# Attention bodies 0 to 4: the gathered expert rows weighted and added by GpSimd instead of VectorE

## What is computed

```python
    x = L0_attn_x
    x = x + 0.5 * _L0_ffn_ref(_layernorm(x, axis=-1), ...)
    x = x + _L0_attn_ref(_layernorm(x, axis=-1), ...)
...
        topk_w, topk_idx = jax.lax.top_k(probs, TOP_K)      # TOP_K = 2 of 8 experts
...
        out = jnp.sum(out * weights[..., None], axis=1)
```

```python
        attn = jax.nn.softmax(jnp.einsum('bhqd,bhkd->bhqk', q, k) * scale, axis=-1)
        out = jnp.einsum('bhqk,bhkd->bhqd', attn, v)
```

## Time and profile before

| | us |
|---|---|
| median of 3 runs | 1469.15 |
| lowest, highest | 1468.4, 1480.79 |
| the profiled execution | 1480.3 |
| its span, first to last instruction | 1478.6 |
| mean granted TensorE clock | 0.951 of full |

### The profile page before, as it was taken

The page is one execution under the profiler, slowest core; times in us unless marked ns, Lnnn a source line. Parts: engine busy times, 40 slices in busy tenths (PEclk is TensorE's granted clock), DMA queues, the critical chain, the costliest instruction groups (busy, mean ns, idle before and its releaser), DMA issues.

```text
span 1478.6 us, 20417 instructions
## 1 busy us (share of the span) xinstructions
PE 1279.2 (87%) x6496; PEld 771.1 (52%) x6496; DVE 1152.3 (78%) x2430; ACT 886.1 (60%) x1402; POOL 517.3 (35%) x757
## 2 busy tenths in 40 slices
PE   5579989778999869979778999989999889899998
PEld 5357768512222322322266777766666345666665
DVE  6377879789999989898456989878786664787875
ACT  5467667437888858868666676733433467434432
POOL 6653326454534524522243334533530110200100
PEclk9779999969999999999989999999999999999999
DMA  8432264342222212210061122263644011055344
GB/s 286 111 96 67 82 214 144 108 123 85 65 67 85 82 46 71 86 36 23 16 257 51 50 72 79 71 151 83 135 90 99 8 32 27 0 117 116 87 88 115
DMA packets 88679, 133.94 MB, mean 91 GB/s; under 512 B 16756, under 2 KB 42836, under 8 KB 87548
## 3 DMA queue, kind: packets, MB, share of 16 engines
q1 hardware_dynamic: 81404, 117.93, 28.3%
q0 software_dynamic: 7168, 14.69, 3.4%
HBM read 82.23 MB, written 47.45 MB: 88 GB/s over the span
## 4 chain that ended last, share of the span: by engine, by line
PE 53%; DVE 24%; issue 9%; ACT 6%; DMA 3%; another core or an unknown queue 1%; POOL 1%; SPq 1%; DVEq 0%; ACTq 0%; POOLq 0%
PE bank L1545 6%; DVE shared L2155 5%; PE pair L894 5%; PE pair L896 5%; PE pair L895 5%; PE bank L2233 4%; PE pair L1457 3%; PE pair L1459 3%; PE pair L1458 3%; DVE shared L950 3%; PE pair L2215 3%; PE pair L2147 3%; ACT shared L2223 2%; DMA shared<-p_coef_rows 1%; PE bank L964 1%
## 5 line engine op out<-in xcount | busy, mean ns | idle before, releaser
L2155 DVE TENSOR_REDUCE shared<-pair 128x2 f32<-128x1024 f32 x256 | 309.7, 1218 | 35.9 <-PE pair L2147 32.7
L2223 ACT ACTIVATE shared<-pair 128x1024 f32<-128x1024 f32 x256 | 260.5, 1021 | 56.8 <-PE pair L2215 54.5
L950 DVE TENSOR_TENSOR shared<-shared 128x512 fp32r<-128x512 f32 x232 | 194.3, 846 | 99.6 <-ACT shared L940 63.2
L894 PE MATMUL pair<-shared 128*128 128x512 f32 x464 | 202.6, 437 | 21.6 <-issue 11.4
L1512 ACT ACTIVATE shared<-pair 128x512 f32<-128x512 f32 x144 | 85.6, 595 | 179.0 <-PE pair L1459 170.1
L896 PE MATMUL pair<-shared 128*128 128x512 f32 x464 | 190.8, 411 | 0.0
L895 PE MATMUL pair<-shared 128*128 128x512 f32 x464 | 190.8, 411 | 0.0
L935 ACT ACTIVATE shared<-pair,shared 128x512 f32<-128x512 f32 x168 | 115.8, 689 | 73.3 <-PE pair L896 67.9
L1457 PE MATMUL pair<-shared 128*128 128x512 f32 x288 | 154.0, 535 | 5.1 <-DVE shared L1467 5.1
L635 POOL DMA_INDIRECT xs_rows<-shared,slots x112 | 114.1, 1019 | 83.6 <-issue 26.9
L2233 PE MATMUL bank<-shared 128*9 128x512 f32 x1024 | 135.9, 603 | 4.5 <-ACT shared L2223 3.7
(11 more groups left out here) (380 smaller groups left out, 2262.2 us busy)
## 6 DMA issues: line engine op xcount, KB each, us to landing
shared<-p_coef_rows SPq DMA_DIRECT2D x64, 512.0 KB
shared<-xs_rows SPq DMA_DIRECT2D x42, 256.0 KB
ys_rows<-shared SPq DMA_DIRECT2D x42, 256.0 KB
w_keep<-shared SPq DMA_DIRECT2D x8, 1024.0 KB
shared<-w_keep SPq DMA_DIRECT2D x16, 512.0 KB
shared<-p_q_parts SPq DMA_DIRECT2D x64, 96.0 KB
shared<-p_k_parts SPq DMA_DIRECT2D x64, 96.0 KB
xs_rows<-shared SPq DMA_DIRECT2D x1, 5376.0 KB, 18.1
```

The costliest lines, as they stand in the source:

```text
L894: nc.tensor.matmul(out_bank, w_hi, x_hi, start=start, stop=False)
L950: nc.vector.tensor_tensor(hl[u % RING][:], hid[u % RING][:], hh[u % RING][:], ALU.subtract).then_inc(s["dve_done"], 1)
L2155: nc.vector.tensor_reduce(mneg[:, i, 2 * c:2 * c + 2], pair_of("max", b, m)[:], AX_X, ALU.max, negate=True).then_inc(s["mx_read"], 1)
L2223: nc.scalar.activation(probs[st % 2][:, 2 * p:2 * p + 2, :], pair_of("exp", b, 2 * st + p)[:], ACT.Exp, scale=scale).then_inc(s["exp_done" ...
```

## The change

In bodies 0 to 4 VectorE's eight fused operations go. GpSimd does the combine in two halves, one for each of the two experts. A half multiplies four 128x128 tiles of the gathered rows in place by the tokens' weights (L321), waits for its own last multiplication (a new semaphore, `scaled`), and adds the four tiles to x by one 128x512 addition (L327), which reports to `x_mix`. The second half's addition also waits for the first's. The first half stands behind the fifth gather and ahead of the split of q, the second behind the last split of maxima and ahead of the split of k. The combine of sequences 0 to 2, outside these bodies, stays on VectorE. The streams of TensorE, ScalarE and SP are the same.

```diff
--- before.py
+++ after.py
@@ -153,7 +153,7 @@
         x_first, x_rest, w_loaded = sem("x_first"), sem("x_rest"), sem("w_loaded")
         rows_loaded, tables_ready = sem("rows_loaded"), sem("tables_ready")
         pool_chain, vecs_ps, vecs_ready = sem("pool_chain"), sem("vecs_ps"), sem("vecs_ready")
-        x_upd, x_mix = sem("x_upd"), sem("x_mix")
+        x_upd, x_mix, scaled = sem("x_upd"), sem("x_mix"), sem("scaled")
         y_stored = [sem(f"y_stored{i}") for i in range(2)]
         gathered = [sem(f"gathered{i}") for i in range(2)]
         xn_ready, xnT_ps, xnT_ready = sem("xn_ready"), sem("xnT_ps"), sem("xnT_ready")
@@ -311,20 +311,20 @@
                 last.then_inc(x_mix, 1)
                 v.wait_ge(x_mix, 2 * (B * occ + b) + k + 1)
 
-        def combine_piece(v, occ, b, j):
-
-            k, i = divmod(j, TILES)
-            t = b * TILES + i
-            if j == 0:
+        def combine_pool(g, occ, b, k):
+
+            if k == 0:
                 per = B // 2 - 1 + b % 2
-                v.wait_ge(gathered[b % 2], 16 * 2 * TILES * (per * occ + b // 2 + b % 2))
-            if j == TILES:
-                v.wait_ge(x_mix, 2 * (B * occ + b) + 1)
-            g = staged[b % 2][:].rearrange("p k (i e) -> p (k i) e", e=E)
-            done = nc.vector.scalar_tensor_tensor(out=x_res[:, t, :], in0=g[:, 2 * i + k, :], scalar=w_tok[:, t, k:k + 1],
-                                                  in1=x_res[:, t, :], op0=ALU.mult, op1=ALU.add)
-            if i == TILES - 1:
-                done.then_inc(x_mix, 1)
+                g.wait_ge(gathered[b % 2], 16 * 2 * TILES * (per * occ + b // 2 + b % 2))
+            rows = staged[b % 2][:].rearrange("p k (i e) -> p (k i) e", e=E)
+            for i in range(TILES):
+                last = nc.gpsimd.tensor_scalar(rows[:, 2 * i + k, :], rows[:, 2 * i + k, :], w_tok[:, b * TILES + i, k:k + 1], None, ALU.mult)
+            last.then_inc(scaled, 1)
+            g.wait_ge(scaled, 2 * (b - 3) + k + 1)
+            if k:
+                g.wait_ge(x_mix, 2 * (B * occ + b) + 1)
+            both = rows.rearrange("p (i k) e -> p i k e", k=2)
+            nc.gpsimd.tensor_tensor(x_res[:, b * TILES:(b + 1) * TILES, :], x_res[:, b * TILES:(b + 1) * TILES, :], both[:, :, k, :], ALU.add).then_inc(x_mix, 1)
 
         def route_consts(g):
 
@@ -2407,16 +2407,12 @@
                 if b + FIRST < B and at == 18:
                     v_dve(v, b + FIRST, bank[7])
                 if b + AHEAD < B:
-                    if at in COMBINE_AT:
-                        combine_piece(v, occ0, b + AHEAD, COMBINE_AT.index(at))
                     if at == 24:
                         norm_stats(v, f0 + b + AHEAD, b + AHEAD)
                     if at == 25:
                         norm_aggr(v, f0 + b + AHEAD)
                 if j == 1:
                     route_dve(v, b, st)
-
-            COMBINE_AT = (13, 15, 16, 17, 19, 20, 21, 23)
 
             def dve_b(v, b, par, first_, last_):
                 for st in range(STEPS):
@@ -2468,10 +2464,14 @@
                 if routes is not None and b:
                     seq_root(g, routes, b - 1)
                 fetch((4, 12))
+                if b + AHEAD < B:
+                    combine_pool(g, occ0, b + AHEAD, 0)
                 if b + FIRST < B:
                     split_pool(g, "q", b + FIRST)
                 fetch((5, 15))
                 msplit_pool(g, b, 3)
+                if b + AHEAD < B:
+                    combine_pool(g, occ0, b + AHEAD, 1)
                 if b + FIRST < B:
                     split_pool(g, "k", b + FIRST)
                 fetch((6, 20))
```

## The result

| | before | after |
|---|---|---|
| median of 6 runs each, us | 1473.78 | 1486.3 |
| lowest, highest | 1468.4, 1480.79 | 1482.41, 1489.21 |
| ratio, 95% interval | | 1.0067 [1.0037, 1.0098] |
| profiled execution, us | 1480.3 | 1486.1 |
| its span | 1478.6 | 1484.4 |

The change makes the kernel slower by 0.67%, some 9.9 us by the ratio; the interval goes from 5.5 to 14.4 us, and the two medians lie 12.5 us apart. The six runs of before are the three that were known and three more; the median of all six is 1473.78, 4.6 us above the 1469.15 from which the forecast started.

What follows compares the result with a forecast made beforehand. No engine was full on average, but VectorE was nearly full inside an attention body, and it and TensorE delayed each other. +5.7 - 1.4 - 0.8 + 2.4 = +5.9 us took the median from 1469.15 to 1475.0, range 1464 to 1487.

Steps and rivals of the forecast that it cites:

- bodies 1 to 3, stall less pieces: TensorE's scores behind L2191 come later, less the price of VectorE's removed combine operations: 1.9 us a body, +5.7 us.
- bodies 1 to 3, clock: TensorE idles before L2191 and its granted clock falls: two falls in three bodies, 1.2 us each, +2.4 us.
- body 0: GpSimd is early before the maxima's split, so its added work hides and VectorE's removed operations show: -1.4 us.
- body 4: GpSimd is early while VectorE's routing holds TensorE back; removed combine operations gain -0.8 us, range -1.5 to 0.
- The place: L2191 in bodies 1 to 3 waits about 3 us for GpSimd's maxima split; none in bodies 0 and 4.
- load: Rival from the experiments: 7.3 us more GpSimd work a body costs wherever it stands, for instance through shared SBUF access.
- C: GpSimd time of one half, four multiplications, gaps and one addition: about 2.9 us, own range 2.6 to 3.5.
- the dear case: Rival at L2191, bodies 1 to 3: GpSimd multiplications cost 884 ns, C is 5.2, +14 us, 1483; chance 0.13.
- the rival of the absorbed stall: The pace picks up behind the stall and no clock falls: about 0 (-2 to +2), 1469; chance 0.15.
- What the pieces were worth: VectorE's eight removed combine operations are worth 0.86 us of an attention body, not their 3.6 us busy time.
- the control: Body 5, without combine and otherwise with the same first 24 units: 25.16 us against 26.02 in body 1.
- The hidden case: Rival: GpSimd's added work hides and the price of VectorE's removed operations simply goes: -4.8 us, 1464.4; chance 0.12.

Runs made afterwards that it cites:

- experiment 5: The changed kernel with the second half's addition left out in bodies 0 to 4, first half in place; attention 431.08 us.
- experiment 6: The changed kernel with both halves behind the last split of maxima and each half's four multiplications made one 128x512 broadcast multiplication; attention 413.85 us, ratio 0.9965.
- experiment 8: The changed kernel with GpSimd combining only in bodies 0 and 4, VectorE as before in bodies 1 to 3; attention 415.99 us, ratio 0.997.
- Experiment 7: The kernel before plus useless GpSimd multiplications of several kinds at its very end; 128x128 by a scalar from memory 0.60 us; attention 420.46 us.
- experiment 4: The changed kernel plus three useless 128x512 TensorE matmuls ahead of L2191 in bodies 1 to 3; attention 422.72 us.
- experiment 3: The changed kernel with each half's four multiplications made one 128x512 two-input multiplication by a broadcast weight; attention 426.53 us.
- experiment 2: The changed kernel with no combine on either engine in bodies 0 to 4, output wrong; attention 416.24 us, ratio 0.9955.
- experiment 1: The changed kernel with both halves moved behind the last split of maxima, ahead of the split of k; attention 424.05 us, ratio 1.0007.

## Why the prediction was right

It gave +5.9 us, 1475.0, in a range of 1464 to 1487; the runs say +9.9 and 1486.3, within the range by 0.7 us. That it is so near the edge has two reasons: the change cost more than forecast, and the median of before moved up by 4.6 us. It gave 87% to a change within 1%. The mechanism, its place and its bodies were right; several sizes were off, and they did not all err the same way. In us of attention:

| | forecast | measured |
|---|---|---|
| bodies 1 to 3, stall less pieces | +5.7 | 3 x (3.65 - 1.34) = +6.9 |
| bodies 1 to 3, clock | +2.4 | 3 x 2.2 = +6.6 |
| body 0 | -1.4 | -1.9 |
| body 4 | -0.8 | -2.9 |
| the rest | 0 | +1.9 |
| all | +5.9 | +10.6 |

- **The place.** L2191 in bodies 1, 2 and 3 waits for the split of the maxima, none does in body 0, and in body 4 the longest wait is 0.73 us, for VectorE. Experiments 5, 6 and 8 show that in these bodies the place is the cause and the load is not.
- **C.** "With the two gaps C = 1.56 + 0.09 + 1.22": the addition was 1.27, near, but a multiplication 0.60 us instead of 0.33. The step that failed is the line drawn through a 128x4 operation and a 128x512 cast, which are not the same operation; "lie on one line" was no argument against the dear case, since any two points do. Experiment 7 has the right slope. C was 3.67, outside the 2.6 to 3.5 of the forecast's own range and inside the wide one. This is +0.8 us a body, 2.3 in all. The page of the Trainium skill that the prediction set beside it (GPSIMD Engine Reference, Engine selection) led to an estimate of 3.6 a half, which came nearer than my rows. But it came there by another way: it calls one-input work on GpSimd nearly as fast as on VectorE, and in experiment 7 the one-input multiplication is the slower one, 1.56 us against 1.04 for the two-input.
- **The stall.** "Every score behind L2191 is that much later: C - 0.12" holds within 0.1 us: 3.65 us for 3.67 in experiment 4, 2.35 for 2.35 in experiment 3. Nothing of it is made up later in the body; the rival of the absorbed stall is out.
- **What the pieces were worth.** 0.86 us a body by the control, 1.34 by experiment 2. The method was sound and the one trace was not: from L2285 to the same exponential body 5 took 25.16 us in the profile that the prediction read, and 24.67 in each of the other nine, as a body without combine does (experiment 2, body 1: 371.90 to 396.57). In the second execution of the same kernel

```profile
587.27 0.68 DVE L2285 TENSOR_TENSOR x_res<-bank,shared 128x512 f32<-128x512 f32 x1
...
611.93 1.02 ACT L2223 ACTIVATE shared<-pair 128x1024 f32<-128x1024 f32 x1 [0.43 <-PE pair L2215]
```

  and body 1 from 375.74 to 401.77, so there the control says 26.03 - 24.66 = 1.37 us. What held body 5 up by 0.5 us in the first profile is not known.
- **The clock.** Two falls of 1.2 us were forecast. There were three, each of 2.2 us in the bodies of the change (experiment 4), and 1.5 where it stayed low for half as long (experiment 3). This term, 6.6 us instead of 2.4, is the larger part of what was missed. In body 1 the sum 3.65 + 2.2 - 1.34 = 4.5 us closes by construction; body 2 is the check, with 4.65 measured.
- **Bodies 0 and 4, and the rest.** Body 0 gained 1.9 us (forecast 1.4). From L2285 of body 3 on, the intervals moved by +6.16, -2.90, -0.48, +0.63 and +0.01. The first holds body 3's own stall and one more fall: the routing of other sequences leaves TensorE idle for 2.57 us there before and after the change; in the earlier trace rows full clock followed, and now

```profile
524.28 0.74 PE L1819 MATMUL bank<-ident,xn 128*128 128x128 f32 x4 [2.57 <-DVE shared L2257]
```

  with 0.50 behind it. This fall is not the change's. In the second execution of the kernel before the same wait came, and the clock was 0.50 behind it:

```profile
509.96 1.11 PE L1819 MATMUL bank<-ident,xn 128*128 128x128 f32 x4 [2.57 <-DVE shared L2257]
...
510.00:513.00 3.00, 3.00 (x16) 0.94 (x16) 1.95 (x2) 1.61 (x2) 0.83 (x4) 0.50 0.00 0
```

  Against that execution the interval moved by 59.64 - 54.89 = +4.75 us, nearly what bodies 1 and 2 did.
- **Body 4** gained 2.9 us, outside the forecast's range of 0 to 1.5. The forecast had GpSimd's work meeting VectorE's routing operations as a loss; it was a gain. TensorE waits there for VectorE's routing operations (L598 to L606, then L2257). Before, they ran beside GpSimd's split of q, and some of them became long; after, the first half's multiplications stand in that place:

```profile
548.75 1.15 POOL L1891 TENSOR_TENSOR shared<-shared 128x512 f32<-128x512 f32 x1
548.78 1.20 DVE L602 TENSOR_TENSOR q_g<-r_g,s_g 128x64 f32<-128x64 f32 x1
```

```profile
552.28 0.25 DVE L602 TENSOR_TENSOR q_g<-r_g,s_g 128x64 f32<-128x64 f32 x1
552.28 2.41 POOL L321 TENSOR_SCALAR staged<-staged,w_tok 128x128 f32<-128x128 f32 x4
```

  The nine operations took 4.56 us before and 2.40 after, and TensorE's wait behind them 5.75 and 3.33. The experiments agree: 2.40 us and 54.73 to 54.81 for the interval wherever the four multiplications stand first (4, 5, 8), 3.6 us and 56.3 to 56.5 where the split of q does and VectorE has no pieces (1, 2, 6). With the two-input multiplication there (3), L602 took 1.10 us beside it, the nine 4.06, and the interval 56.88. So 'load' has a true part, in another body, and there the change won by it.

The rival of dear multiplications had the direction and a price too high (C = 5.2; its own terms add up to 5.1). The hidden case, -4.8 us, is what experiment 6 came near to, by moving and shortening the work.

## What to carry to other kernels

An engine at 35% can still be the one that is waited for: before work is moved to it, look in its own timeline for the next result that somebody needs, and how late that result may be (here next to nothing at one place and some 5.5 us at the next: 4.7 us of work fitted between them, 7.3 did not). The price of work taken off a full engine is not its busy time; leave it out in one run and see (here 1.34 us of 3.6). A control read from one execution can be off by a good part of what it is to measure (here 0.5 us of 1.34): read it in a second one. And a new wait of TensorE is paid twice if its clock falls behind it.

## What the runs showed that I had not expected

- On GpSimd a multiplication of f32 by one scalar per partition takes 0.60 us for 128x128 and 1.56 for 128x512, with an immediate 0.52 and 1.49, while a two-input multiplication by a broadcast operand takes 1.04 us for 128x512.
- The granted clock was 0.50 behind each idle time of 4.16 us, behind two of three of 2.77 us, and behind the three of 2.04 us in experiment 1. The wait before L1819 in body 3 (2.57 us; 2.08 in experiment 1) is in all ten profiles: in two, before and experiment 6, full clock followed, in eight 0.50. The idle time alone does not tell whether it falls.
- A two-input operation of VectorE on 128x64 took 0.25 us beside GpSimd's multiplications by one scalar per partition, 1.20 beside its addition of two 128x512 operands and 1.10 beside its multiplication by a broadcast one (L602 in body 4).
- TensorE did 2.84 us of matmuls of no use in each of three bodies, and attention became 7.2 us shorter (experiment 4).
